# Rounding of x's fp4 quantisation moved from VectorE to GpSimd, as three operations in place of two

## What is computed

```python
def fp4_quant_dequant(x):          # blocks of 16 along the last dim
    scale = max(max(abs(xb)) / 6.0, 1e-12)
    xn = xb / scale
    idx = searchsorted(MID, abs(xn))           # MID = .25 .75 1.25 1.75 2.5 3.5 5
    return GRID[idx] * sign(xn) * scale        # GRID = 0 .5 1 1.5 2 3 4 6

x = x + xattn(ctx_2048, layernorm(x), mask, mask, W_src, b_src, W_tgt, b_tgt, W_out, b_out)   # 8 heads of 16
xq = fp4_quant_dequant(layernorm(x))
h = silu(xq @ quant(w_gate).T) * (xq @ quant(w_up).T)        # 352 wide
out = x + fp4_quant_dequant(h) @ quant(w_down).T
```

## Time and profile before

| | |
|---|---|
| Median of 3 runs | 225.11 us (224.66 to 225.33) |
| Profiled execution, its own time | 227.31 us |
| Its span, first to last instruction | 225.5 us |
| Mean granted TensorE clock | 0.968 of full speed |
| Busy: PE, DVE, POOL, ACT | 189.2, 175.6, 139.5, 132.9 us |

### The profile page before, as it was taken

One profiled execution on the slowest core, in us unless ns is written; L12 is line 12 of the kernel. 1 busy time (PEld: TensorE's weight loads), 2 busy tenths in 40 slices (PEclk: granted clock), 3 DMA queues, 4 the chain that ended last, 5 costly groups with the idle time before them and its releaser, 6 DMA issues.

```text
span 225.5 us, 5688 instructions
## 1 busy us (share of the span) xinstructions
PE 189.2 (84%) x2045; PEld 140.5 (62%) x2045; DVE 175.6 (78%) x391; ACT 132.9 (59%) x264; POOL 139.5 (62%) x203
## 2 busy tenths in 40 slices
PE   0779899699699999999999947688898998989454
PEld 0255759549459586684977714466586676767443
DVE  7356977839977979767699869799989889898641
ACT  2366979559468778787777433155365555555421
POOL 5288372635799764819455868975758575755820
PEclk9999999889979999999999996699999999999999
DMA  6999832102000000000000000000110101011011
GB/s 202 309 310 271 281 91 88 58 3 93 3 0 4 3 0 4 3 3 0 3 4 0 4 0 0 0 0 3 49 45 2 47 3 47 0 48 44 7 47 47
DMA packets 13665, 11.97 MB, mean 53 GB/s; under 512 B 766, under 2 KB 10558, under 8 KB 13630
## 3 DMA queue, kind: packets, MB, share of 16 engines
q1 hardware_dynamic: 13078, 11.29, 16.1%
q10 hardware_dynamic: 560, 0.33, 0.5%
HBM read 9.52 MB, written 2.10 MB: 52 GB/s over the span
## 4 chain that ended last, share of the span: by engine, by line
POOL 31%; PE 25%; issue 21%; DVE 10%; ACT 5%; DMA 4%; POOLq 1%; SPq 1%; DVEq 0%; ACTq 0%
POOL wq_y L358 9%; POOL hq L373 8%; PE bank L881 5%; PE bank L869 4%; POOL xn L254 4%; DMA b_out<-in_bo 4%; POOL xq_all L288 2%; DVE st L571 2%; POOL rs L244 2%; PE bank L875 2%; PE bank L949 2%; PE bank L832 2%; ACT val L419 2%; DVE den L608 2%; DVE x_all L626 1%
## 5 line engine op out<-in xcount | busy, mean ns | idle before, releaser
L373 POOL TENSOR_TENSOR hq<-wq_u,sch 128x704 f32<-128x704 f32 x16 | 22.6, 1411 | 20.8 <-DVE wq_u L754 20.8
L937 PE MATMUL bank<-guT,xqT 128*128 128x352 f32 x64 | 25.8, 486 | 3.2 <-DVE hh L727 3.2
L541 ACT COPY hT<-bank 128x384 f32<-128x384 f32 x32 | 15.3, 479 | 22.1 <-PE bank L949 22.1
L961 PE MATMUL bank<-wdT,hT 128*128 128x128 f32 x192 | 26.8, 276 | 1.3 <-ACT hT L541 0.8
L949 PE MATMUL bank<-ident,hq 128*128 128x128 f32 x96 | 16.9, 287 | 12.9 <-POOL hq L373 12.9
L949 PEld LDWEIGHTS bank<-ident,hq 128*128 128x128 f32 x96 | 11.8, 145 | 22.0 <-POOL hq L373 18.2
L940 PE MATMUL bank<-guT,xqT 128*128 128x352 f32 x64 | 25.5, 481 | 0.0
L961 PEld LDWEIGHTS bank<-wdT,hT 128*128 128x128 f32 x192 | 24.0, 192 | 1.9 <-ACT hT L541 1.1
L869 PE MATMUL bank<-cT,wsT 128*128 128x512 f32 x32 | 19.4, 740 | 6.3 <-DMA cT<-in_ctxT 6.3
L358 POOL TENSOR_TENSOR wq_y<-hh,ivh 128x704 f32<-128x704 f32 x16 | 22.2, 1389 | 3.5 <-DVE ivh L742 2.0
L473 ACT ACTIVATE mask_bc<-bank 128x352 f32<-128x352 f32 x32 | 14.7, 460 | 13.6 <-PE bank L937 13.4
(11 more groups left out here) (117 smaller groups left out, 493.6 us busy)
## 6 DMA issues: line engine op xcount, KB each, us to landing
cT<-in_ctxT SPq DMA_DIRECT2D x8, 512.0 KB, 5.9
x_all<-in_x SPq DMA_DIRECT2D x8, 256.0 KB, 5.9
mask_bc<-in_mask_rows SPq DMA_DIRECT2D x8, 256.0 KB, 6.5
out_y<-mask_bc SPq DMA_DIRECT2D x8, 256.0 KB, 2.2
wsT<-in_WsT ACTq DMA_DIRECT2D x1, 256.0 KB, 4.0
w_all<-in_wg SPq DMA_DIRECT2D x1, 176.0 KB
w_all<-in_wu SPq DMA_DIRECT2D x1, 176.0 KB
w_all<-in_wd SPq DMA_DIRECT2D x1, 176.0 KB
```

What stands on the lines that cost most here:

```text
L373: nc.gpsimd.tensor_tensor(hq[i][:, :, 0:I].rearrange("p t (n k) -> p t n k", k=BLK), rh[i][:, :, :].rearrange("p (t n) k -> p t n k", t=2) ...
L541: nc.scalar.copy(hT[n % 2][:, :, :].rearrange("p c t -> p (c t)"), t_bank[place % 2][:, 0:IP]).then_inc(t_ok, 1)
L937: nc.tensor.matmul(gu_bank[2 * n % 3][:, 0:I], xqT[g % 2][:, t], guT[:, 0, :], start=True, stop=True).then_inc(pe_g, 1)
L961: last = nc.tensor.matmul(d_bank[:, j * P:(j + 1) * P], hT[n % 2][:, c, :], wdT[:, c, :], start=(c == 0), stop=(c == 2))
```

## The change

`s3_round` goes from DVE's program. POOL gets `round_of`, which computes the same values in three operations: the bound `c2 = max(min(a2, BIG), c)`, the sum `u2 = c2 + y2` and the difference `r2 = c2 - u2`. `min(a2, BIG)` changes no value. Between the three POOL waits for its own result. There is one more tile, `c2`, and one more semaphore. In the attention, `round_of(k-3)` is the last thing in POOL's step k, for k = 3 to 7; in the FFN it stands right ahead of `xq_of` at u = 0, 2 and 4.

```diff
@@ tiles and semaphores
+        c2 = sb("c2", [P, TILES * NB_X, BLK])
...
@@ POOL
+            def round_of(g):
+                pool.wait_ge(a2_ok, g + 1)
+                pool.wait_ge(y2_ok, g + 1)
+                past(pool, r2_ok, g)
+                nc.gpsimd.tensor_scalar(c2[:, :, :], a2[:, :, :], BIG, FLOOR * MAGIC, ALU.min, ALU.max).then_inc(c2_ok, 1)
+                pool.wait_ge(c2_ok, g + 1)
+                nc.gpsimd.tensor_tensor(u2[:, :, :], c2[:, :, :], y2[:, :, :], ALU.add).then_inc(u2_ok, 1)
+                pool.wait_ge(u2_ok, g + 1)
+                past(pool, xq_ok, g)
+                nc.gpsimd.tensor_tensor(r2[:, :, :], c2[:, :, :], u2[:, :, :], ALU.subtract).then_inc(r2_ok, 1)
...
                 if on(g1 + 3):
                     rstd1_of(g1 + 3)
+                if on(g4) and g4 < NG - 3:
+                    round_of(g4)
...
                 if u == 0:
+                    round_of(NG - 3)
                     xq_of(NG - 3)
                     scales2_of(NG - 2)
                     y_of(NG - 2)
...
                 if u == 2:
+                    round_of(NG - 2)
                     xq_of(NG - 2)
                     scales2_of(NG - 1)
                     y_of(NG - 1)
                 if u == 4:
+                    round_of(NG - 1)
                     xq_of(NG - 1)
@@ DVE
-            def s3_round(g):
-                dve.wait_ge(a2_ok, g + 1)
-                dve.wait_ge(y2_ok, g + 1)
-                nc.vector.scalar_tensor_tensor(out=u2[:, :, :], in0=a2[:, :, :], scalar=FLOOR * MAGIC, in1=y2[:, :, :],
-                                               op0=ALU.max, op1=ALU.add).then_inc(u2_ok, 1)
-                dve.wait_ge(u2_ok, g + 1)
-                past(dve, xq_ok, g)
-                nc.vector.scalar_tensor_tensor(out=r2[:, :, :], in0=a2[:, :, :], scalar=FLOOR * MAGIC, in1=u2[:, :, :],
-                                               op0=ALU.max, op1=ALU.subtract).then_inc(r2_ok, 1)
...
-                if on(g4) and g4 < NG - 3:
-                    s3_round(g4)
...
-                if m == 0:
-                    s3_round(NG - 3)
...
-                if m == 4:
-                    s3_round(NG - 2)
...
-                if m == 8:
-                    s3_round(NG - 1)
```

More of the change, by code:

```diff
@@ L155, in xattn_ffn @@
                              "av_ok", "updT_ok", "x2_ok"))
-        stat2, aggr2, var2, nm2_ok, rstd2, xn2_ok, am2_ok, sc2_ok, up2_ok, iv2_ok, y2_ok, a2_ok, u2_ok, r2_ok, xq_ok = (
+        stat2, aggr2, var2, nm2_ok, rstd2, xn2_ok, am2_ok, sc2_ok, up2_ok, iv2_ok, y2_ok, a2_ok, c2_ok, u2_ok, r2_ok, xq_ok = (
             sem(n) for n in ("stat2", "aggr2", "var2", "nm2_ok", "rstd2", "xn2_ok", "am2_ok", "sc2_ok", "up2_ok",
-                             "iv2_ok", "y2_ok", "a2_ok", "u2_ok", "r2_ok", "xq_ok"))
+                             "iv2_ok", "y2_ok", "a2_ok", "c2_ok", "u2_ok", "r2_ok", "xq_ok"))
         pe_x0, x0_ok, pe_t, t_ok, pe_g, pe_u, pe_dn = (
```

## The result

The changed kernel takes 242.01 us in the median of 4 runs (238.96 to 245.12), against 225.22 of the kernel before: 1.067 times, 95% interval 1.054 to 1.081. Medians here are of all runs and ratios of the fast ones alone, those within 1.5% of the fastest of the same kernel, which is why 1.067 is less than 242.01 / 225.22. The profiled execution took 245.12 us with a span of 243.3, so it is some 3 us above the median. The profiles differ by up to 3 us in how early PE gets to step 2, before any round. So stages are compared from milestone to milestone inside one execution.

A forecast was written before the change was run, and what follows sets the result against it. No single bound: PE sets the steady attention steps, DVE the FFN after its waits for POOL's `up2`. Attention 12.0, FFN 7.4 and clock 1.5 sum to 20.9 us, on 225.11 giving 246.0; range 235 to 256.

The forecast's parts named there:

- mechanism of place: POOL's order: the round is queued ahead of work others wait for, so POOL's later idle time is no cover.
- The bound: First operation of POOL's round, `min` then `max` on one input: taken as 1.8 us.
- the rival with a cheap bound: POOL's bound costs 0.61 us like the copy, the round 3.3, no clock fall: 235 us in all, chance 0.23.
- R: Length of one round on POOL, three operations and two handovers: about 4.5 us, ends 2.9 and 5.4.
- Attention: Rounds delay the openings of steps 4 to 8: +4.5 for step 3, +3.3 step 4, +4.2 steady steps, together +12.0 us.
- R - 1.2: Loss in attention step 4, where POOL's own work leaves almost no slack: +3.3 us.
- 10.47 + R: Length of steady attention steps 5 to 7 after the change: 15.0 us against 13.58, +1.4 each.
- TensorE's clock: One fall to the 1.2 GHz level in attention, after PE's longest wait, ahead of step 5: +1.5 us.
- The FFN: Rounds delay `up2` and `y_unit(5)`, so DVE's product for tile 14 comes later and stays so: +7.4 us.
- R + 0.2 - 0.7: FFN delay of iv(6): the round plus handovers, less the first unit's earlier start; 4.0 us.
- the way over `y_unit(5)`: FFN: POOL's 9.1 us between `y_unit(4)` and `y_unit(5)` hold the buffer for DVE's tile 14 product: +7.4 us.
- DVE's relief: Rounding taken from DVE, worth 0.7 + 0.7 + 1.4 + 2.4 = 5.2 us in the FFN, nothing in attention.

The follow-up runs named there:

- Run 11: Changed kernel with POOL's bound computed twice (same values), a round of 4.0 us in place of 3.3: 249.93 us, 8.5 above the changed kernel run again.
- run 9: Changed kernel with useless matmuls on PE ahead of its wait, four in step 4 and two in step 5: 238.79 us, beside 241.47 for the changed kernel.
- run 7: Kernel with only groups 5 to 7 rounded on POOL, the others on DVE, and group 7's rounding moved late: 235.0 us, before 226.76.
- run 4: Changed kernel with the bound left out, so a round has two operations and computes another rounding: 235.34 us, ratio 1.036 to the kernel before.
- runs 3, 8 and 9: Changed kernel edited: 3, attention rounds behind POOL's copy for PE, 239.09 us; 8, nine and four useless PE matmuls in steps 4 and 5, 243.05; run 9 above.
- run 5: Changed kernel with the rounding left out on both engines (another result): 222.96 us, ratio 0.987 to the kernel before.
- run 2: Changed kernel with groups 0 to 4 rounded on DVE as before, only groups 5 to 7 on POOL: 235.76 us, ratio 1.044.

## Why the prediction was right, and where it was wrong

The direction, the size within range (242.0 in 235 to 256, with 246 forecast) and the mechanism of place held. Two terms were off and cancelled in part, so that the total came as near as it did is luck.

- **The bound: wrong.** I took 1.8 us from the slope of two small rows with a `min`. It takes 0.61, as the rival with a cheap bound had it, and the Trainium skill's page GPSIMD Engine Reference, section 4.1, which calls work with one input roughly line-rate. So R is 3.3, not 4.5. What that page of the Trainium skill says of two inputs, about twice VectorE's time, agrees with the measured 1270 ns against 693 on DVE.
- **By my own sum with R = 3.3 the time would have been 235.** The median was 7 us more, so the cheap rival was right about the part and wrong about the whole. These 7 us are 5.7 in the FFN and 1.6 for the clock, below.
- **Attention: mechanism right, 12.0 forecast, 5.2 without the clock measured.** Step 3 costs 2.9 where R alone gives 3.3. The difference is a gain that the sum left out: POOL's `rs` near the end of the step took 1.47 us beside DVE's rounding, and 1.02 us now. Step 4: 2.3 where R - 1.2 gives 2.1. Steady steps: 0 where 10.47 + R gives 0.2. Run 11 moves them with R: from the spread of step 3 to that of step 8 it takes 80.3 us, the changed kernel 76.3.
- **TensorE's clock: right as a cost, right in place and size for attention.** One fall was counted, ahead of step 5, at 1.5 us; run 9 shows 1.6 there. The term left out the FFN.
- **The FFN: the step that failed.** I had 7.4 with R = 4.5, which is 3.9 with R = 3.3; it is 9.6. The two waits for `up2` came out as worked: iv(6) 2.7 late (R + 0.2 - 0.7 gives 2.8), iv(7) 6.0 (2 x 3.5 - 0.7 gives 6.3). The lead from DVE's own relief showed little: tile 10 was 5.4 late where 3.9 was due, after DVE had waited 1.15 us ahead of tile 9 for PE's products at the low clock (0.64 from 164 to 166 us, after PE had stood 4.43 us for `hq`). And the way over `y_unit(5)` was not the one that bound. POOL's backlog behind `round_of(7)` held `hq_unit(3)` first, PE's transposes stand ahead of gate and up of tile 13, and those ran at the low clock: 3 us more. I had followed POOL's queue to DVE and not to PE. In run 7, without that backlog, this stretch was 3.6 us shorter, and runs 4 and 11 move it with the length of the round.
- **The end of the span** is 1.1 us longer behind the last product (18.0 against 16.9 us). It is a fall of the clock that is not the change's: the last twelve matmuls of `down` took 2.77 us in place of 1.67, and in runs 3, 8 and 9, with the same FFN, they took 1.67. The spans' 17.8 are then 2.0 ahead of step 3 and 1.3 in it, 2.3, 1.6, 9.6 and 1.1, within rounding. What the change itself costs is 2.9 + 2.3 + 1.6 + 9.6 = 16.4, beside 16.8 between the medians and 15 by the ratio of 1.067.
- **DVE's relief** was put at no more than 5.2 us if all else were free; run 5 gives 3. Of the 2.8 counted up to the waits for `up2` 1.0 shows. Group 7's 2.4 shows in full at tile 9 and is 1.7 from tile 11 on. Even with a round at no cost the change had little to win.
- **Contention** of DVE and POOL was no large part: the mean of DVE's `uph` went from 256 to 290 ns, 0.5 us over all sixteen.

Open: how much of run 7's 3.6 us shows in the time of many executions, and why a stand of PE is followed by the lower clock in some executions and not in others.

## What to carry to other kernels

Before moving work to an engine with idle time, look at what stands behind the new place in that engine's order and who waits for it, then follow that waiter's own queue one engine further. Here POOL was idle 38% of the span, and a round of 3.3 us still cost 2.9 us where POOL was the last to come. A busy engine is worth relieving only where something waits for it: 12 us of DVE's work were worth 3. And moving the work past one waiter finds the next, so check each consumer of the queue before reordering.

## What the runs showed of the hardware that was not expected

- POOL's `tensor_scalar` with `min` and `max` over 128x512 takes 612 ns, the same as the copy of that size (611 ns), though with a `min` it takes 325 ns at 32 and 361 ns at 44 elements a partition. Two small rows are no base for a slope.
- Stands of PE of 2.25 us ahead of step 5 and 2.66 and 4.43 us in the FFN were followed by the 1.2 GHz level, one of 1.42 us (run 4) was not. Other stands went either way. Ahead of step 3 PE stood 1.83 us in the profile of the kernel before and 2.18 in run 4's, and the clock fell (0.50); it stood 1.11 us in run 2's and 1.36 in the changed kernel's, and the clock stayed. Before the last `down` it stood 2.24 us in the kernel before without a fall and 2.23 in the changed kernel with one. So the length of the last stand alone does not tell.
- Such a fall cost 1.7 us in step 3 (16.22 against 14.54 us), 1.6 in step 5 and 1.1 in the last `down`. In run 9, four and two useless matmuls ahead of the waits kept steps 4 and 5 at the full level, and 1.6 us of step 5 were won by it.
